# A macaron block on one core: the place of a weight reload on SP, and of routing steps and weights on VectorE

## What is computed

```python
x = x + 0.5 * _L0_ffn_ref(_layernorm(x), gate_w, gate_up_proj, down_proj)
x = x + _L0_attn_ref(_layernorm(x), w_qkv, w_out)
x = x + 0.5 * _L0_ffn_ref(_layernorm(x), gate_w, gate_up_proj, down_proj)

# attention, 16 heads of 16
scores = jnp.einsum('bqhd,bkhd->bhqk', q, k)
scores = jnp.where(causal_mask, scores, NEG)
attn = softmax(scores)
out = jnp.einsum('bhqk,bkhd->bqhd', attn, v).reshape(b, s, HIDDEN) @ w_out

# mixture: 16 experts of width 128, two per row
p = sigmoid(x @ gate_w.T);  p = p / sum(p)
w, idx = top_k(p, 2);       w = w / sum(w)
y_e = (silu(x @ gate_e) * (x @ up_e)) @ down_e
out = sum over the two chosen experts of w * y_e
```

## Time and profile before

| | |
|---|---|
| median of 3 runs | 817.87 us (816.4 to 819.97) |
| profiled execution | 817.24 us |
| its span | 815.4 us |
| mean granted clock of TensorE | 0.929 |
| busy: PE, DVE, ACT, POOL | 665.5, 528.8, 418.3, 417.1 us |
| DMA, mean over the span | 148 GB/s |

### The profile page before, as it was taken

The page is one execution under the profiler, slowest core; times in us unless marked ns, Lnnn a source line. Parts: engine busy times, 40 slices in busy tenths (PEclk is TensorE's granted clock), DMA queues, the critical chain, the costliest instruction groups (busy, mean ns, idle before and its releaser), DMA issues.

```text
span 815.4 us, 17364 instructions
## 1 busy us (share of the span) xinstructions
PE 665.5 (82%) x5367; PEld 530.3 (65%) x5384; DVE 528.8 (65%) x1644; ACT 418.3 (51%) x1024; POOL 417.1 (51%) x557
## 2 busy tenths in 40 slices
PE   2638999887868999999999899896775656998990
PEld 2438889776746777777777566664434546887880
DVE  7888644333666888788888988855486313343678
ACT  1534566555414555555555555555564524565660
POOL 4124555555342555455555542357677674555551
PEclk9958999999978999999999999999877787999996
DMA  8793456555553444444444333246115343555979
GB/s 255 246 295 96 137 159 170 155 137 144 136 152 100 117 119 121 119 117 112 116 119 114 98 87 86 74 139 204 60 69 173 100 153 123 153 146 145 308 260 325
DMA packets 96920, 121.04 MB, mean 148 GB/s; under 512 B 12352, under 2 KB 83280, under 8 KB 96848
## 3 DMA queue, kind: packets, MB, share of 16 engines
q1 hardware_dynamic: 82992, 81.82, 33.5%
q0 software_dynamic: 13824, 38.29, 16.2%
q10 hardware_dynamic: 32, 0.02, 0.0%
HBM read 51.99 MB, written 38.34 MB: 111 GB/s over the span
## 4 chain that ended last, share of the span: by engine, by line
PE 62%; DVE 17%; issue 5%; another core or an unknown queue 4%; DMA 4%; ACT 4%; POOL 2%; SPq 2%; DVEq 0%; ACTq 0%; POOLq 0%
PE bank L1208 9%; PE bank L1516 8%; PE bank L613 6%; PE bank L1220 5%; PE bank L1523 4%; PE bank L674 4%; PE bank L635 4%; PE bank L660 4%; PE bank L694 3%; DVE mx L1020 3%; PE bank L620 3%; PE bank L1198 2%; PE bank L638 2%; PE bank L1507 2%
## 5 line engine op out<-in xcount | busy, mean ns | idle before, releaser
L525 POOL TENSOR_SCALAR_AFFINE_SELECT pr<-pr 128x512 f32<-128x512 f32 x128 | 81.4, 658 | 135.6 <-ACT pr L790 132.5
L1020 DVE TENSOR_REDUCE mx<-bank 128x2 f32<-128x512 f32 (+1 forms) x192 | 127.7, 683 | 29.6 <-PE bank L638 21.7
L790 ACT ACTIVATE pr<-bank 128x512 f32<-128x512 f32 x192 | 105.8, 603 | 40.0 <-PE bank L660 22.6
L1356 POOL DMA_INDIRECT spare<-normed,source x80 | 76.9, 962 | 89.4 <-PE bank L1507 43.6
L1166 POOL DMA_INDIRECT returned<-shared,source x80 | 77.5, 969 | 62.4 <-DVE shared L1296 41.7
L1208 PE MATMUL bank<-xeT,shared 128*128 128x128 f32 x640 | 90.0, 286 | 10.8 <-ACT xeT L1261 6.8
L1208 PEld LDWEIGHTS bank<-xeT,shared 128*128 128x128 f32 x640 | 82.7, 202 | 12.3 <-issue 12.0
L1516 PE MATMUL bank<-xeT,shared 128*128 128x128 f32 x640 | 87.6, 281 | 1.2 <-ACT xeT L1643 1.0
L1516 PEld LDWEIGHTS bank<-xeT,shared 128*128 128x128 f32 x640 | 80.6, 198 | 2.1 <-issue 2.0
L1289 DVE TENSOR_TENSOR act_rows<-bank,act_rows 128x128 f32<-128x128 f32 x80 | 23.2, 290 | 89.0 <-ACT act_rows L1277 55.3
L432 POOL DMA_INDIRECT gathered_rows<-grouped,slot x64 | 67.4, 1053 | 16.1 <-issue 12.3
(11 more groups left out here) (344 smaller groups left out, 1496.3 us busy)
## 6 DMA issues: line engine op xcount, KB each, us to landing
shared<-parts SPq DMA_DIRECT2D x154, 128.0 KB
grouped<-pr SPq DMA_DIRECT2D x80, 132.0 KB
spare<-grouped SPq DMA_DIRECT2D x80, 132.0 KB
spare<-parts SPq DMA_DIRECT2D x70, 128.0 KB
shared<-returned SPq DMA_DIRECT2D x32, 256.0 KB
normed<-shared SPq DMA_DIRECT2D x8, 512.0 KB, 3.9
wgu_sb<-_L_ffn_gate_up_proj_dram SPq DMA_DIRECT2D x8, 512.0 KB, 8.7
wd_sb<-in_L_ffn_down_proj_dram SPq DMA_DIRECT2D x8, 512.0 KB
```

The source lines that it names most:

```text
L525: nc.gpsimd.affine_select(out=m, in_=m, compare_op=ALU.is_ge, fill=0.0, base=0, pattern=[[0, 4], [1, P]], channel_multiplier=-1).then_inc( ...
L790: nc.scalar.activation(dst.rearrange("p h n -> p (h n)"), bank[n % 3][:, :], ACT.Exp).then_inc(at["exp_ready"], 1)
L1020: nc.vector.tensor_reduce(mx[:, u, h0:h0 + nh], bank[3 + n % 2][:, :].rearrange("p (h k) -> p h k", h=nh), AX.X, ALU.max).then_inc(at["max ...
L1356: nc.gpsimd.indirect_dma_start(xe[r], None, normed, bass.IndirectOffsetOnAxis(source[:, j:j + 1], 0)).then_inc(xe_loaded[r], 16)
```

## The change

SP issues the transfer of the maxima of batch 14 ahead of the reload of the down weights, not behind it. In class 0, the routing takes one step at every place, except for two steps at three places. The weights of the chosen experts are computed behind the slots of each class: class 0's still between maxima, class 2's at the end of its routing, class 1's after it (the generator is handed from `attn_vector` to `last_vector`). No computation is added or removed.

```diff
                 if kind == MAX:
+                    after(sp, at["nmaxT_ready"], b + 1)
+                    after(sp, at["scoreT_done"], 3 * G * (b - BUFS + 1))
+                    sp.dma_start(qT[b % BUFS][ROWS:ROWS + 3, :, :], nmaxT[:, :]).then_inc(at["maxed"], 16)
                     if b == B - 2:
                         sp.wait_ge(l["slots_ready"], 1)
                         for g in range(0, E, 4):
                             sp.dma_start(wd_sb[:, g:g + 4, :], down[g:g + 4].rearrange("e i h -> i e h")).then_inc(wd_loaded, 16)
-                    after(sp, at["nmaxT_ready"], b + 1)
-                    after(sp, at["scoreT_done"], 3 * G * (b - BUFS + 1))
-                    sp.dma_start(qT[b % BUFS][ROWS:ROWS + 3, :, :], nmaxT[:, :]).then_inc(at["maxed"], 16)
...
             nc.vector.tensor_tensor(picks[:, ts, :], tb.pick[0], tb.pick[1], ALU.add).then_inc(l["picks_ready"], 1)
-            yield from chain(dve, nc.vector.tensor_tensor(wsum[:, ts], top[0][:, ts], top[1][:, ts], ALU.add))
-            yield from chain(dve, nc.vector.reciprocal(wrec[:, ts], wsum[:, ts]))
-            for j in range(TOPK):
-                nc.vector.scalar_tensor_tensor(out=weight[:, ts, j], in0=top[j][:, ts], scalar=0.5, in1=wrec[:, ts],
-                                               op0=ALU.mult, op1=ALU.mult)
             yield "counts"
...
+            yield "placed"
+            yield from chain(dve, nc.vector.tensor_tensor(wsum[:, ts], top[0][:, ts], top[1][:, ts], ALU.add))
+            yield from chain(dve, nc.vector.reciprocal(wrec[:, ts], wsum[:, ts]))
+            for j in range(TOPK):
+                nc.vector.scalar_tensor_tensor(out=weight[:, ts, j], in0=top[j][:, ts], scalar=0.5, in1=wrec[:, ts],
+                                               op0=ALU.mult, op1=ALU.mult)
...
         ROUTE_FROM, BEFORE_LAST = (CUT[1] // 2, 5), 23
+        STEPS_AT = {(CUT[1] // 2, 5): 2, (CUT[1] // 2, 7): 2, (CUT[1] // 2 + 1, 7): 2}
...
                     if ROUTE_FROM <= (b, n) and b < B - 1:
-                        for _ in range(1 + n % 2):
+                        for _ in range(STEPS_AT.get((b, n), 1)):
                             advance(b, n)
...
                     elif b == B - 1 and n == 4:
-                        for _ in routing[1]:
-                            pass
+                        for reached in routing[1]:
+                            if reached == "placed":
+                                break
                         experts_of(dve, 0)
...
             batches(DVE_TURN, part)
+            return routing[1]
...
             experts_of(dve, 1)
+            for _ in weights_left:
+                pass
```

More of the change, by code:

```diff
@@ L1280, in last_scalar, with last_vector @@
                     read_expert(j + 3)
-        def last_vector(dve):
+        def last_vector(dve, weights_left):
             def expert_tile(j):
@@ L1978, in _ @@
             first_vector(dve)
-            attn_vector(dve)
-            last_vector(dve)
+            last_vector(dve, attn_vector(dve))
 _INS = ["L0_attn_x", "L0_attn_w_qkv", "L0_attn_w_out", "L0_ffn_gate_w", "L0_ffn_gate_up_proj", "L0_ffn_down_proj"]
```

## The result

| | before | changed |
|---|---|---|
| median | 817.98 us (813.33 to 821.15, 19 runs) | 812.93 us (807.57 to 818.05, 19 runs) |
| ratio | | 0.9934, 95% interval 0.9914 to 0.9954 |
| profiled execution, its span | 817.24, 815.4 us | 814.88, 813.1 us |
| mean granted clock | 0.929 | 0.923 |

The change is faster by 0.66%, some 5.4 us, with an interval from 3.8 to 7.0. The forecast was 8.3, so direction and range were right and the size was too large. Single executions of either kernel lie up to 5.4 us from their median.

A forecast was written before the change was run, and what follows sets the result against it. PE was taken to bound the undisturbed attention stage, with DVE's routing steps and the wait for batch 14's transfer adding time. 817.24 - 5.5 - 2.5 - 0.3 = 808.9, forecast as 809.0; range 805.5 to 813.5.

The forecast's parts named there:

- The reload: Stage at 565.23: issuing batch 14's maxima transfer ahead of the reload removes PE's wait; -5.5 us, bounds -3 to -5.7.
- With PE at 567.3 the first mask is wanted at 570.0: Stage at 565.23: POOL is free at 569.86, so it caps the gain at 5.6 and takes nothing from 5.5.
- The rival of ScalarE held by POOL's scatters: Stage at 565.23: exponentials held behind POOL's scatters cost 3, first scatters 1 more; total 813, chance 0.2.
- The steps: Routing stages of class 0: spreading steps saves pauses and moves steps to idle places; -2.5 us, bounds 0 and -4.5.
- The stage at 518.27 should not grow: Sign to look for: the routing stage at 518.27, 25.39 us long before, takes in new steps without growing.
- the pauses in pairs: Class 0 routing on DVE: a pair costs 0.11 to 0.12 more than two single steps; some 0.9 us go.
- The weights: Routing of classes 1 and 2: weights behind the slots gain 0.2 and 0.1; -0.3 us, bounds 0 and -1.
- only the transfer counts: Rival: spread steps only move DVE's backlog into the stage at 518.27; total 811.4, chance 0.17.
- The "slower" rival: Last block: one more longest ScalarE wait costs 8.8 and a second 3.5; total 821.5, chance 0.03.
- the part past 615 lasts longer than before by more than 2 us: Sign of being wrong: the last block, past 615, grows by more than 2 us.

The follow-up runs named there:

- p1: The kernel before, unchanged, run and profiled once more; ratio 0.9982 to the kernel before.
- r1: The kernel before with only the transfer of batch 14's maxima moved ahead of the reload; median 814.09 us, ratio 0.9957.
- r2: The changed kernel with the routing steps of before, so reload and weights moved but steps not; median 814.01 us, ratio 0.9946.
- r3: The kernel before with only the routing steps spread, reload and weights as before; median 817.02 us, ratio 0.9981.
- q2: The changed kernel with two scatters of batch 14 left to the last block and the routing steps of before; median 806.37 us, ratio 0.9938.
- q4: The changed kernel with two of the seven scatters ahead of batch 14's first mask left to the last block; median 805.41 us, ratio 0.9907.
- r4: The changed kernel with the reload one stage later, behind the transfer of batch 15; median 814.66 us, ratio 0.9959.
- q1: The changed kernel, unchanged, run and profiled once more; median 805.01 us, ratio 0.9928 to the kernel before on the same chip.
- q3: The changed kernel with the weights of the chosen experts in their old place, behind the picks; median 803.45 us, ratio 0.9896.
- s1: The changed kernel with two of the seven scatters ahead of POOL's first mask put between masks instead, in every turn; ratio 0.9961.

## Why the prediction was right in sign and too large

**The reload.** Forecast -5.5, of which 4.8 in S6 (25.27 to 20.5) and 0.7 in S5, by the earlier issue. S6 is 25.27, 26.49 and 25.62 in the three profiles without the swap, mean 25.79, and 22.70, 24.04, 22.75, 22.79, 22.67 and 23.65 in the six with it and with the scatters in place, mean 23.10: -2.7. S5, with the old steps, went from 21.57 (before) or 20.94 (p1) to 20.83 (r1, r2): -0.1 to -0.7, for in p1 the issues of the reload ended just as the transfer's data were ready. Together -2.8 to -3.4; the total of r1 says -3.5 (-5.6 to -1.3). The step that failed is "With PE at 567.3 the first mask is wanted at 570.0, when POOL has just come free. So POOL caps the gain at 5.6 and takes nothing from 5.5." PE's score came 2.8 behind the transfer, as forecast, in three of the six profiles and some 1.6 later in the others, and POOL came free 5.4 to 5.5 behind it, as forecast; but the first mask came 7.7 behind it in all six, not 5.5, because ScalarE's exponentials came late. I checked that POOL would be free, and took ScalarE's 0.65 behind PE from a place where no scatter was in progress. The rival of ScalarE held by POOL's scatters had the mechanism and, with 3 us, nearly the size of what S6 gave back (2.2). That its 813 is the measured median is partly luck: its extra 1 for the first scatters did not come as it was put, and the steps brought less than it assumed. Its chance of 0.2 was too low: its own rows, 5.21 and 8.78, had no other explanation, and against it stood a single counterexample.

**The steps.** Forecast -2.5. S3: -2.2 forecast, -1.8 measured in every pair of kernels. S1: -0.7 forecast, -0.7 to -1.2 at full clock (-1.1 in most) and nothing at 0.87. S2: +0.1 forecast, 0 measured. S4 and S5 with the later slots: +0.3 forecast, and measured, among the profiles with the swap, as the mean of eight with late slots, 46.64, less that of three with early ones, 46.08: +0.6. Single profiles lie up to 1.1 us from these means. Together -2.3 or -1.2, by the clock. The totals say -1.6 in r3 (-3.7 to +0.6) and -1.0 in q2 against q4, and can't choose between the two. "The stage at 518.27 should not grow" was the wrong sign to look for: it fell by 2.4 because a wait left it for its neighbour. On the pauses in pairs no run decides. The step pair in the changed kernel's S1 starts 0.45 apart (454.44 to 454.89), as in the earlier trace rows, so the row still disagrees with the Trainium skill (VectorE: DVE Perf Modes, section The DRAIN you can't avoid), by which the semaphore costs nothing extra in a row of eight copies; but how much of S3's 1.8 is pauses, and how much the places of the steps, was not separated.

**The weights.** Forecast -0.3. The slots of class 1 come 21.24 to 21.44 behind batch 15's transfer where they stand ahead of the weights (changed, r2, r4, q1), and 21.75, 21.92, 21.94, 22.97 and 23.05 where they stand behind (before, q3, p1, r3, r1): -0.3 at least, and up to -1.8 between r1 and r2. In the five profiles with scatters moved they come at 21.88 to 23.66, ahead of the weights as they are. I put -0.5, an estimate that no total shows.

**The sum** is -2.8 to -3.4 for the reload, -1.2 or -2.3 for the steps and -0.5, so -4.5 to -6.2, and -5.4 was measured. So the direction was right by the mechanism of both parts, and the result lies near the upper end of the range mostly because the reload brought 3 and not 5.5. The profiled executions differ by only 2.4, with a last block that was 4.06 longer in the changed one. Against the rival "only the transfer counts" stand S3 and, at full clock, S1; the total of r3, which takes in no change, can't settle it. The "slower" rival is not seen in the totals. The sign "the part past 615 lasts longer than before by more than 2 us" came in the first profile and would have misled, had there been no second profile of both kernels.

## What to carry to other kernels

When one wait is taken out of a stage, check every engine behind it at its new time, and take the distances between engines from rows where the same neighbours are busy, here GpSimd with a run of indirect transfers. Compare sums of neighbouring stages before a gain in one of them is believed. A difference in a part that the change can't touch asks for a second profile of both kernels before it gets a cause.

## What the runs showed of the hardware

**ScalarE and GpSimd's indirect transfers.** In S6 of all six profiles that have the swap and the run of seven scatters, ScalarE stands with its inputs ready and starts its second group of exponentials 1.43 to 1.58 us behind the end of POOL's last scatter; in s1 it starts all four 1.16 behind it. With two or four scatters fewer there is no such gap. It is not a rule that ScalarE stands still while GpSimd issues such transfers. The very first exponential starts 0.42 to 0.46 behind PE's score in r4 and q3, during the last scatter:

```profile
561.17 0.38 PE L660 MATMUL bank<-spare 115*128 115x256 bf16 x2
...
561.59 0.60 ACT L790 ACTIVATE pr<-bank 128x512 f32<-128x512 f32 x1 [3.42 <-issue]
563.59 1.57 ACT L790 ACTIVATE pr<-bank 128x512 f32<-128x512 f32 x3 [1.41 <-PE bank L660]
...
561.16 0.96 POOL L468 DMA_INDIRECT grouped<-gathered_rows,slot  x1 [0.30 <-issue]
```

(q3). In q2 all four start 0.25 behind the end of the run (561.36), at 561.61, and for batch 15 of the changed kernel the exponentials start 0.43 behind PE's score, at 587.35, while POOL goes on issuing until 589.53. Two rivals are out by the traces. The reload's traffic made no difference (r4). And no loading of code is seen: the hold of q1 (564.34 to 565.92) lies in a stretch, 556 to 570, in which the profile has no packet of an instruction queue. What tells the places apart, and by what path GpSimd holds ScalarE, stays open; a scatter of fewer bytes in the same run, which could tell the issuing from its own traffic, was not tried.

**TensorE's clock.** S1 was granted 0.87 in seven of fourteen profiles, 0.93 in one and 1.00 in the others, with the same orders ahead of it. At 0.87 the old steps take 0.8 to 1.3 us more than at 1.00 and the new ones 1.6 to 2.3, so the change gains nothing in S1 on such an execution. In S6 the eight projection matmuls ahead of the first score (L694) take 2.10 us in the changed kernel, r2 and q1, whose S6 was granted 1.00, and 3.46 to 3.79 in r1, r4 and q3, which were granted 0.86 to 0.93; the score comes some 1.6 later there and the first mask does not. What decides it wasn't found.

**The last block** took 219 to 232 us in fourteen profiles of kernels that run nearly the same work there, a spread larger than the whole effect of the change.
